# A decoder layer on one core: in each second step of the attention, masking, exponentials and sinks go ahead of the division and the rotation

## What is computed

```python
x = x + attn(layernorm(x))                       # x: (16, 256, 512)
x = x + conv_mix(ctx, ctx, layernorm(x))         # long convolution over 512 taps, 32 heads of 8
x = x + ffn(layernorm(x))                        # the factors, summed, times 1/sqrt(8), plus a bias

def attn(x):                                     # 32 query heads, 8 key/value heads of 64
    q, k, v = split(x @ qkv_w.T + qkv_b)
    q, k = rope(q), rope(k)
    logits = q k^T / 8, masked to j <= i and j > i - 128
    m = max(logits); e = exp(logits - m)
    w = e / (sum(e) + exp(sink - m))
    return (w @ v) @ out_w.T + out_b
```

## Time and profile before

| | us |
|---|---|
| median of 3 runs (lowest, highest) | 1990.8 (1989.84, 1991.06) |
| the profiled execution's own time | 1991.15 |
| its span in the trace | 1989.3 |
| TensorE busy in the span | 1945.1 |
| VectorE busy | 1549.4 |
| ScalarE busy | 932.2 |
| GpSimd busy | 826.0 |

### The profile page before, as it was taken

One profiled execution on the slowest core, in us unless ns is written; L12 is line 12 of the kernel. 1 busy time (PEld: TensorE's weight loads), 2 busy tenths in 40 slices (PEclk: granted clock), 3 DMA queues, 4 the chain that ended last, 5 costly groups with the idle time before them and its releaser, 6 DMA issues.

```text
span 1989.3 us, 44846 instructions
## 1 busy us (share of the span) xinstructions
PE 1945.1 (98%) x15500; PEld 1601.7 (81%) x15500; DVE 1549.4 (78%) x4948; ACT 932.2 (47%) x3481; POOL 826.0 (42%) x947
## 2 busy tenths in 40 slices
PE   6899999999999999999999999999999999999899
PEld 6688888888888888888888888888887777777687
DVE  5777777777777777777777777777777899999887
ACT  4554555555555555555555555555544222222333
POOL 3444434333333333333333333333332666666554
PEclk9999999999999999999999999999999999999999
DMA  6146211111112122121111111111104533333343
GB/s 213 46 118 142 72 54 55 65 54 55 55 54 75 44 97 76 55 89 62 54 55 54 54 54 55 54 65 54 54 33 167 183 103 93 93 93 93 106 142 121
DMA packets 71538, 162.20 MB, mean 82 GB/s; under 512 B 6656, under 2 KB 15232, under 8 KB 71184
## 3 DMA queue, kind: packets, MB, share of 16 engines
q1 hardware_dynamic: 62720, 142.48, 21.4%
q0 software_dynamic: 3840, 8.39, 2.3%
q10 hardware_dynamic: 4752, 8.46, 1.1%
HBM read 108.96 MB, written 50.41 MB: 80 GB/s over the span
## 4 chain that ended last, share of the span: by engine, by line
PE 91%; DVE 3%; issue 2%; ACT 2%; POOL 1%; DMA 0%; DVEq 0%; SPq 0%; ACTq 0%; POOLq 0%
PE banks L534 22%; PE banks L596 18%; PE banks L1180 16%; PE banks L573 9%; PE banks L549 9%; PE banks L559 6%; PE banks L1408 5%; PE banks L527 4%; ACT pr L673 1%; PE banks L484 1%; PE banks L1398 1%; PE banks L473 1%; PE banks L1392 1%; DVE pr L891 1%; DVE m L867 0%
## 5 line engine op out<-in xcount | busy, mean ns | idle before, releaser
L673 ACT ACTIVATE pr<-pr,mx 128x128 f32<-128x128 f32 x1024 | 399.0, 391 | 353.1 <-DVE mx L891 353.0
L752 POOL TENSOR_TENSOR m<-m,rope_sb 128x512 f32<-128x512 f32 x160 | 206.3, 1289 | 513.9 <-ACT m L660 513.9
L534 PE MATMUL banks<-xTh,wh 128*128 128x256 f32 x1280 | 376.4, 294 | 2.3 <-DVE xTl L851 1.4
L534 PE MATMUL banks<-xTl,wh 128*128 128x256 f32 x1280 | 363.0, 284 | 0.0
L534 PE MATMUL banks<-xTh,wl 128*128 128x256 f32 x1280 | 362.6, 283 | 0.0
L1180 PE MATMUL banks<-kv,tap 128*128 128x288 f32 x1280 | 318.4, 408 | 4.3 <-issue 1.5
L1180 PEld LDWEIGHTS banks<-kv,tap 128*128 128x128 f32 x1280 | 238.1, 190 | 83.9 <-issue 23.3
L534 PEld LDWEIGHTS banks<-xTh,wh 128*128 128x128 f32 x1280 | 246.2, 192 | 4.0 <-DVE xTl L851 1.8
L900 DVE TENSOR_TENSOR den<-ac,es 128x4 f32<-128x4 f32 x256 | 51.7, 202 | 253.9 <-ACT es L676 253.7
L534 PEld LDWEIGHTS banks<-xTl,wh 128*128 128x128 f32 x1280 | 246.5, 193 | 0.0
L534 PEld LDWEIGHTS banks<-xTh,wl 128*128 128x128 f32 x1280 | 246.1, 192 | 0.0
(11 more groups left out here) (110 smaller groups left out, 3825.6 us busy)
## 6 DMA issues: line engine op xcount, KB each, us to landing
tap<-padded_taps SPq DMA_DIRECT2D x64, 256.0 KB, 3.3
kk<-in_ctxt SPq DMA_DIRECT2D x64, 192.0 KB, 3.4
x_in<-in_x SPq DMA_DIRECT2D x16, 512.0 KB, 3.8
xt_split<-xTh SPq DMA_DIRECT2D x16, 512.0 KB, 2.6
xt_split<-xTl SPq DMA_DIRECT2D x16, 512.0 KB, 3.6
xb<-in_x SPq DMA_DIRECT2D x16, 512.0 KB, 4.6
factors<-in_factors POOLq DMA_DIRECT2D x8, 1024.0 KB, 8.6
x_part_rows<-x SPq DMA_DIRECT2D x16, 512.0 KB, 3.0
```

The costliest lines, as they stand in the source:

```text
L534: last = pe.matmul(bank[:, h * T:(h + 1) * T], w[:, n, c, h * P:(h + 1) * P], a[:, s, c, :], start=(c == 0 and i == 0), stop=(c == KD - 1 ...
L673: act.activation(pr[:, s, a, cols], pr[:, s, a, cols], ACT.Exp, bias=mx[:, s, i:i + 1], scale=-1.0, accum_out=ac[:, s, i:i + 1])
L752: pool.tensor_tensor(m2[:, s], m2[:, s], rope_sb[:, 1 if i == 0 else 0, 1:3], ALU.mult).then_inc(sin_ready, 1)
```

## The change

In every slot with j = 1, `mask_min` (VectorE) goes ahead of `divide`, `mask_transposed` and `turned`, `exps` (ScalarE) goes ahead of `bent`, and `sinks_shifted` (GpSimd) goes ahead of `rotate`. Slots with j = 0 keep the order, and the special order of sweep 1 goes. In the first body: the output weights' pieces 6 to 9 are split in slots 0, 2, 4 and 6 of the second window instead of slots 4 to 7 of the first; the queue's loads are reordered to fit; the transposes of the second x's first tile go from slot 2 to slot 3; in slots 6 and 7 of the first window (p == 3) the unit goes ahead of `p_transposes`; and splits stand ahead of the exponentials on ScalarE there too.

```diff
--- before.py
+++ after.py
@@ -256,9 +256,13 @@
 
         return y.sweep == 0 and y.number != HM - 1
 
+    X_FIRST = {3: 0, 4: 1}
+    X_AT = {2: 0, 4: 1}
+
     def x_next(y, p, j):
 
-        return p % 4 in (1, 2) and j == 0 and fresh(y, p)
+        tiles = X_FIRST if y.first and p < 4 else X_AT
+        return tiles.get(2 * (p % 4) + j) if fresh(y, p) else None
 
     def late(y, lag, p):
 
@@ -305,8 +309,11 @@
     def split_now(y, p, j):
 
         k = 2 * p + j
-        if y.first and k < NS - 2:
+        if y.first and k < NU - 2:
             return [(2 + k, 2 + k)]
+        if y.first and k in (8, 10, 12, 14):
+            n = NU + (k - 8) // 2
+            return [(n, n)]
         if y.number == HM - 1 and k in (9, 10, 12, 14, 15):
             n = (9, 10, 12, 14, 15).index(k)
             return [(NS + n, n)]
@@ -398,18 +405,18 @@
             x_load(2)
             sp.wait_ge(lo_done, 6)
             load_raw(7)
-            sp.wait_ge(lo_done, 7)
-            load_raw(8)
             x_save(1, 1)
-            sp.wait_ge(lo_done, 8)
-            load_raw(9)
             sp.dma_start(tap0[:, 0:1], ssm_pad[:, P - 1:P], allow_slow_non_contiguous=True).then_inc(tap_in, 16)
             sp.dma_start(tap0[:, 1:2], dcoef).then_inc(tap_in, 16)
             sp.dma_start(pad_dram, ssm_pad).then_inc(tap_in, 16)
+            sp.wait_ge(lo_done, 7)
+            load_raw(8)
+            x_load(3)
+            sp.wait_ge(lo_done, 8)
+            load_raw(9)
+            x_save(2, 0)
             sp.wait_ge(lo_done, NS)
             sp.dma_start(xb[:], rows(x, 0)).then_inc(xb_landed, 16)
-            x_load(3)
-            x_save(2, 0)
 
         def body(y):
             m = y.m
@@ -605,13 +612,16 @@
         def body(y):
             for p in range(8):
                 for j in range(2):
+                    n = unit_of(p, j)
+                    ahead = y.first and p == 3
+                    if ahead:
+                        unit(y, p, n)
                     if y.here(p, 3):
                         p_transposes(y, p, j)
-                    n = unit_of(p, j)
-                    if n is not None and not y.drain:
+                    if n is not None and not y.drain and not ahead:
                         unit(y, p, n)
-                    if x_next(y, p, j):
-                        x_transposes(y.window(p) + 1, p % 4 - 1)
+                    if x_next(y, p, j) is not None:
+                        x_transposes(y.window(p) + 1, x_next(y, p, j))
                     if j == 0 and y.here(p, 2):
                         scores(y, p)
                     u, jj = (p - 4, 1) if j == 0 else (p - 3, 0)
@@ -706,24 +716,22 @@
                 for j in range(2):
                     if y.here(p, 3):
                         p_evac(y, p, j)
+                    if j == 1 and y.here(p, 2):
+                        exps(y, p, j)
                     n = unit_of(p, j)
                     if n is not None and n != V_UNIT and not y.drain:
                         bent(y, p, rope_index(n), unit_bank(y, p, n))
-                    if x_next(y, p, j):
-                        x_high(y.window(p) + 1, (p // 4 + 1) % 2, p % 4 - 1, y.m + p // 4)
+                    if x_next(y, p, j) is not None:
+                        x_high(y.window(p) + 1, (p // 4 + 1) % 2, x_next(y, p, j), y.m + p // 4)
                     u, jj = (p - 4, 1) if j == 0 else (p - 3, 0)
                     if y.here(u, 0):
                         o_high(y, u, jj)
                     if x1_here(y, p, j) is not None:
                         x1_evac(y.window(p) - 3, x1_here(y, p, j))
-                    if not y.first:
-                        for i, n in split_now(y, p, j):
-                            split_high(i, n)
-                    if y.here(p, 2):
+                    for i, n in split_now(y, p, j):
+                        split_high(i, n)
+                    if j == 0 and y.here(p, 2):
                         exps(y, p, j)
-                    if y.first:
-                        for i, n in split_now(y, p, j):
-                            split_high(i, n)
                 if y.drain and p in (4, 6):
                     conv.first_queries(act, p // 2 - 2)
                 if y.drain and p == 4:
@@ -780,6 +788,8 @@
         def body(y):
             for p in range(8):
                 for j in range(2):
+                    if j == 1 and y.here(p, 2):
+                        sinks_shifted(y, p, j)
                     n = unit_of(p, j)
                     if n is not None and n != V_UNIT and not y.drain:
                         rotate(y, p, rope_index(n))
@@ -789,8 +799,8 @@
                         for t in range(NT):
                             last = pool.tensor_tensor(xb[:, t, :], xb[:, t, :], bo_sb[:], ALU.add)
                         last.then_inc(xb_ready, 1)
-                    if y.here(p, 2):
-                        if y.first and p == 2 and j == 0:
+                    if j == 0 and y.here(p, 2):
+                        if y.first and p == 2:
                             pool.wait_ge(c_in, 16 * NCONST)
                         sinks_shifted(y, p, j)
                     for i, n in split_now(y, p, j):
@@ -965,15 +975,14 @@
                         conv.first_sums(dve)
                     if residual_tile(y, p, j) is not None:
                         residual(y, p, residual_tile(y, p, j))
+                    if j == 1 and y.here(p, 2):
+                        mask_min(y, p, j)
                     u, jj = (p - 3, 1) if j == 0 else (p - 2, 0)
                     if y.here(u, 0):
                         divide(y, u, jj)
                     if y.here(p, 3):
                         mask_transposed(y, p, j)
                     n = unit_of(p, j)
-                    early = 2 * (p % 4) + j in (1, 3) and not fresh(y, p) and not y.drain
-                    if early:
-                        mask_min(y, p, j)
                     if n is not None and not y.drain:
                         if y.first and n == V_UNIT and p < 4:
                             dve.wait_ge(c_in, 16 * NCONST)
@@ -981,9 +990,9 @@
                             v_evac(y, p)
                         else:
                             turned(y, p, rope_index(n), unit_bank(y, p, n))
-                    if x_next(y, p, j):
-                        x_low(y.window(p) + 1, (p // 4 + 1) % 2, p % 4 - 1)
-                    if y.here(p, 2) and not early:
+                    if x_next(y, p, j) is not None:
+                        x_low(y.window(p) + 1, (p // 4 + 1) % 2, x_next(y, p, j))
+                    if j == 0 and y.here(p, 2):
                         mask_min(y, p, j)
                     u, jj = (p - 4, 1) if j == 0 else (p - 3, 0)
                     if y.here(u, 0):
```

## The result

The changed kernel takes **2031.88 us** (median of 4 runs, 2030.1 to 2032.37) beside 1990.32 us for the kernel before on the same chip (4 runs, 1989.36 to 1991.06). The ratio is 1.0208, with a 95% interval of 1.0196 to 1.0221: slower by 41.6 us, where 30 were forecast. The spans, 2030.5 and 1989.3 us, differ by 41.2.

What follows compares the result with a forecast made beforehand. TensorE, busy 1945.1 of 1989.3 us, was taken as the bound, with gains possible only in the first two windows. Terms 19.2 + 1.0 + 2.0 + 4.6 + 6.2 + 4.5 - 5 - 2 = +30.5 gave 2021 us, range 2004 to 2038.

Steps and rivals of the forecast that it cites:

- slot 7 mechanism: In slot 7, VectorE reaches `mask_min` late, so `exps`, `bent` and `turned` run late and slot 0's unit waits.
- first body: First two windows: shorter TensorE waits against copies moved to the second window; sum -5 us, at best -12, at worst +3.
- x1 transposes: Sweep 1, slot 2: they wait for a layer norm's end behind `turned`; 0.35 x 13 = +4.5 us.
- (a): Slot 7 to slot 0, sweep 0: unit waits 1.6 us per window, 19.2 in windows 2 to 13; +1.0 and +2.0 elsewhere.
- (b): Slot 1 to slot 2, sweep 0: x transposes wait 0.35 us for the bank, 13 windows, +4.6.
- (c): Slots 3 and 5: later chain hidden by the unit's 3.0 us; 0.3 each if that cover were gone.
- (d): Sweep 1: unit after slot 7 0.4 us late, +6.2 over 15 windows; x1 transposes in slot 2, +4.5.
- small waits up to 180 us: Small TensorE waits of 98 to 180 us, and some in the drain, go: -2 us.
- collisions: Rival: slot 0's divisions meet GpSimd's moved rotation, about 0.9 us longer; 22 us more if transposes are reached, 2043; 4%.
- split of window 15: Window 15 has no statistics but a weight split in their place; windows 14 and 15 together 0.4 + 1.6 = +2.0 us.
- The clock: Rival: new waits in every window bring TensorE to half clock, 36 to 84 us more, 2057 to 2105; 4%.
- The leads of the steady windows: Rival, faster side: they absorb the later `bent`, only the first body's gain stays, 1984 us; 9%.

Runs made afterwards that it cites:

- e2: Changed kernel with the old order in slot 7 alone, on all three engines; slots 1, 3 and 5 keep the new one: 1996.98 us, ratio 1.0034.
- e5: Changed kernel with the residual moved behind `mask_min` on VectorE in slot 7: 2020.05 us, ratio 1.0153.
- e1: Changed kernel with `bent` ahead of `exps` on ScalarE again; VectorE and GpSimd keep the new order: 1998.97 us, ratio 1.0044.
- e7: Changed kernel with the old order in slot 1 alone: 2036.3 us, ratio 1.0223.
- e6: Changed kernel with the old order in bodies 7, 8, 9 (windows 14 to 19) and the drain: 2020.0 us, ratio 1.0153.
- e3: Kernel before with only the first body's other edits; old order in all slots with j = 1: 1990.12 us, ratio 0.9999.
- h2: Changed first body, new order on all three engines, `exps` ahead of `bent` too, in the first body only, except its last slot: 1989.77 us, ratio 0.9999.
- h1: Changed first body, new VectorE and GpSimd order there only, except its last slot; `bent` ahead of `exps` everywhere: 1984.17 us, ratio 0.9967.
- e4: Kernel before with the new order in all slots with j = 1, the first body's other edits undone: 2034.16 us, ratio 1.0217.

## Why the prediction was right in kind and too low

It forecast slower by the slot 7 mechanism, and the kernel is slower by it, within the range. The sum was 30.5 (with 0.4 x 15 taken as 6.2; it is 6.0, so 30.3), the measured 41.2 by the spans. The lags say where the 11 us lie:

| stretch | predicted | measured |
|---|---|---|
| first body, up to window 1 | -5 | -1.9 |
| windows 1 to 13 | 1.0 + 11 x 1.6 + 12 x 0.35 - 2 = 20.8 | 25.9 |
| 13 to 18 | 1.6 + 0.35 + 2.0 + 2 x 0.4 = 4.8 | 9.1 |
| 18 to 31 | 13 x (0.4 + 0.35) = 9.8 | 5.4 |
| behind 31 | 0 | 2.7 |

That the total came within the range is in part luck: 4.5 us were charged for x1 transposes that lose nothing, and they stand in for part of what was missed elsewhere. The range's upper end is also not what the stated bounds give: with all of them at their ends the sum comes to about 2040, not 2043.

**(a), slot 7 to slot 0.** Right in place and size: 1.59 against 1.6, every hand-over to within 0.04. e2 confirms the place, e5 that the start of `mask_min` sets it, e1 that ScalarE's order makes it.

**(b), slot 1 to slot 2.** 0.28 against 0.35, and 0.21 to 0.24 is left by it when slot 7 is undone (e2). But a term by itself it is not: e7 removes it and loses more elsewhere.

**(c), slots 3 and 5.** Right in the steady windows: between 180 and 700 us, TensorE's only waits are those of the three rows at the end of this document, and the 11 long ones are slot 0's. Wrong in windows 2 and 3, as shown below. e7 too makes visible how thin the cover is.

**(d), sweep 1.** The 0.4 at slot 7 is exact. The 4.5 for the x1 transposes is 0: in e2, slots 1 and 2 keep the new order and sweep 1 loses nothing. The bound "between 0 and 0.45" had it. The step that failed is the 1.44 us carried over for the layer norm's end beside GpSimd's addition. In its new place it no longer meets GpSimd and takes 0.54 (the kernel before, then the changed one; busy us, mean ns, idle time before):

```profile
L834 DVE TENSOR_SCALAR xn<-x,mv,rs 128x512 f32<-128x512 f32 x32 | 28.9, 905 | 1.6 <-POOL rs L742 1.6
```

```profile
L844 DVE TENSOR_SCALAR xn<-x,mv,rs 128x512 f32<-128x512 f32 x32 | 17.1, 538 | 1.6 <-POOL rs L750 1.6
```

**Windows 2 and 3.** They cost 4.45 and 2.79 us instead of 1.87, and the 2 us that the small waits up to 180 us were to give back did not come. This is where collisions reached TensorE. In slot 2 of both windows the division meets GpSimd's two additions to `xb`. Window 3 (timelines of VectorE, GpSimd and TensorE, changed kernel):

```profile
165.00 4.10 DVE L915 TENSOR_TENSOR pr<-pr,rden 128x512 f32<-128x512 f32 x1
```

```profile
165.49 3.05 POOL L800 TENSOR_TENSOR xb<-xb,bo_sb 128x512 f32<-128x512 f32 x2
```

```profile
175.76 0.60 PE L566 MATMUL banks<-id_sb,pr 128*128 128x128 f32 x4
...
177.22 0.63 PE L480 MATMUL banks<-id_sb,xn 128*128 128x128 f32 x4 [0.86 <-issue]
```

The division takes 4.10 us (3.55 in window 2) and ends 0.56 behind GpSimd's additions. VectorE then works without a gap up to `mask_min` of slot 3, so `exps`, `bent` and `turned` of slot 3 are late, and slot 4's x transposes start 1.46 behind the others instead of 0.43: 1.03 lost in each of the two windows. In window 3 this is the whole excess of 0.9. In window 2 more is lost, with a wait of 1.03 for masked transposes at 98.62; what makes it was not tried. The chain is read from the timelines; no run takes the collision out by itself.

**Windows 13 to 18.** 9.1 against 4.8. 3.0 of the excess are the two stretches at half clock, and 1.5 are window 17: the prediction counted the split of window 15 in slot 7 and not that of window 17, which makes 2.0 of a step put at 0.4 to 0.8.

**Behind window 31.** It was put down as a small gain; it loses 2.7, at full clock, and other kernels with the new order in it lose up to 6.6 (e2, 3.2 of it clock), while e6, with the old one, loses nothing.

**The first body.** The signs of its parts were right: e3 shows a lead of 3.5 in window 0 of which 1 remains. The size is uncertain in itself: e5 and e6, whose first two windows run the same code, are 4.1 to 4.2 ahead at window 1 where the changed kernel's trace is 1.9 ahead. What was missed is that `exps` ahead of `bent` costs there too, 5.6 us by h2 less h1; the prediction credited the shorter chain of exponentials and never charged the later unit.

**The rivals.** The clock did not fall in every window, as that rival had it: from 98 us on, 28 of the unit's 30 waits, of 0.15 to 1.31 us, are followed by no fall. But it did fall twice, at 785.0 and 880.6, each time behind the two waits of windows 15 and 17, and cost 3.0 us. The leads of the steady windows did not absorb the change. Collisions reached TensorE in windows 2 and 3, for about 2 us; the rival asked for 22.

**Open.** The other 1.5 us of window 2; what exactly makes the drain's 2.7; 1.0 of the difference between e2's drain and the changed kernel's that is not clock; and why the clock fell in window 17 of the changed kernel and not of e4, behind the same waits.

## What to carry to other kernels

On an in-order engine, the call that frees a bank for the bounding engine belongs ahead of longer work for a later consumer; put behind it, it inherits the wait and the length of that work, here 1.34 and 1.65 us on ScalarE. Before a reorder, write down slot by slot how long before its consumer each bank is free, with all that stands ahead in the special bodies too, and reorder only where the bounding engine idles: the same order that costs 44 us everywhere is part of the fastest kernel here (h1) when VectorE's and GpSimd's share of it is confined to the first body. Test slots together, since a wait taken out of one can come back in another. And before a loss is put down to an order, look at the granted clock of its stretch: here the clock made 3.0 of 9.1 us in one place and 3.2 of 6.6 in another.

## What the runs showed of the hardware

The divisions, L915, from the page of the changed kernel (busy us, mean ns):

```profile
L915 DVE TENSOR_TENSOR pr<-pr,rden 128x512 f32<-128x512 f32 x256 | 278.9, 1089 | 8.8
```

They took 735 ns in the mean before, with the same shape and count: 90.8 us more, as much as VectorE's whole growth of 90.5; what the other groups gain and lose cancels. Alone, a division takes 0.69; beside GpSimd's rotation it takes 1.57 (timeline of VectorE, then of GpSimd, changed kernel):

```profile
445.65 1.57 DVE L915 TENSOR_TENSOR pr<-pr,rden 128x512 f32<-128x512 f32 x1
```

```profile
445.38 1.29 POOL L769 TENSOR_TENSOR qT<-m,m 128x512 f32<-128x512 f32 x1
```

The division ends at 447.22, 0.55 behind GpSimd's end (445.38 + 1.29 = 446.67), about what it takes alone. The 4.10 us of window 3 end 0.56 behind two GpSimd additions in a row. The Trainium skill (SBUF — State Buffer, Who interferes with whom) says that two such operations shut each other out for a whole instruction; these rows agree. Not expected was how little it matters in the steady windows. A drawn-out division would show as a wait of the transposes that follow it, L566. From 180 to 700 us, in windows like the one of these rows, TensorE's waits in the changed kernel are these and no others:

```profile
PE banks L541 <- DVE m L877: 14.4, 11, 1.3
PE banks L480 <- issue: 0.6, 2, 0.3
PE banks L566 <- DVE pT L923: 0.2, 1, 0.2
```

A group's mean that grows by half cost at most 0.2 us there, and a gap of 1.3 us that hardly moves an engine's busy share cost most of the 2%. Only where the division was held for 3.6 to 4.1 us, in windows 2 and 3, did it cost TensorE 1.03 us each.

TensorE's granted clock fell to 0.50 for 3.4 us behind waits of 0.33 and 1.31 us within 2 us (880.60 to 884.00), and the same pair of waits in e4 was followed by 1.00, as was a pair of 1.03 and 1.30 us at 98.62 and 100.55 in the changed kernel. Such a stretch cost 1.5 us.
